# Row maxima of the first batch's scores taken ahead of a block's hidden product on VectorE

## What is computed

```python
def ffn(x):        # 8 experts, top 2
    scores = softmax(xt @ router_w); weights, idx = top_k(scores, 2)
    h = gelu(x @ w1[e]) * (x @ v1[e])        # D = 128, F = 352
    y = h @ w2[e]
    return sum_k weights_k * y[idx_k] + bias
def attn(x):       # 16 heads of 8
    q, k, v = rope(qkv)
    attn = q @ k.T * scale + alibi
    out = softmax(attn) @ v
    return out @ proj_w.T + proj_b
x = x + 0.5 * ffn(layernorm(x))
x = x + attn(layernorm(x))
x = x + 0.5 * ffn(layernorm(x))
```

## Time and profile before

| | |
|---|---|
| median of three runs | 499.47 us |
| the profiled execution's own time | 502.36 us |
| its span, first to last instruction | 500.5 us |
| TensorE busy in the span | 439.6 us (88%) |
| TensorE weight loads | 367.2 us (73%) |
| VectorE | 318.6 us (64%) |
| ScalarE | 249.1 us (50%) |
| GpSimd | 236.9 us (47%) |
| mean granted TensorE clock | 0.972 |

### The profile page before, as it was taken

The page is one execution under the profiler, slowest core; times in us unless marked ns, Lnnn a source line. Parts: engine busy times, 40 slices in busy tenths (PEclk is TensorE's granted clock), DMA queues, the critical chain, the costliest instruction groups (busy, mean ns, idle before and its releaser), DMA issues.

```text
span 500.5 us, 10906 instructions
## 1 busy us (share of the span) xinstructions
PE 439.6 (88%) x3447; PEld 367.2 (73%) x3447; DVE 318.6 (64%) x935; ACT 249.1 (50%) x585; POOL 236.9 (47%) x321
## 2 busy tenths in 40 slices
PE   1999989989889884998989898989788999999990
PEld 1878878888878663676867676767557988888880
DVE  3767869778556645384868585847436675545672
ACT  4745644364443534354565546454664554554441
POOL 7267796564523214034435253514254568643341
PEclk9999999999999989798999899999998999999996
DMA  9981121223220102121212111110022123223522
GB/s 245 284 116 55 48 75 45 79 71 97 70 60 24 43 22 54 33 65 34 55 53 54 45 48 40 45 43 22 7 87 64 53 67 112 59 60 96 149 79 79
DMA packets 50633, 35.51 MB, mean 71 GB/s; under 512 B 5754, under 2 KB 47706, under 8 KB 50538
## 3 DMA queue, kind: packets, MB, share of 16 engines
q1 hardware_dynamic: 45140, 23.90, 19.3%
q0 software_dynamic: 4784, 10.54, 6.3%
q10 hardware_dynamic: 656, 0.40, 0.3%
HBM read 15.37 MB, written 13.01 MB: 57 GB/s over the span
## 4 chain that ended last, share of the span: by engine, by line
PE 58%; DVE 8%; issue 7%; ACT 5%; POOL 4%; DMA 3%; ACTq 1%; SPq 1%; POOLq 0%; DVEq 0%
PE bank L1582 6%; PE bank L1485 5%; PE bank L1606 5%; PE bank L1621 5%; PE bank L1478 5%; PE bank L1467 4%; PE bank L1468 3%; PE bank L1469 3%; PE bank L1585 3%; PE bank L1586 3%; PE bank L1609 2%; PE bank L1610 2%; POOL yp L538 2%; PE bank L1457 2%; DVE nm L1260 2%
## 5 line engine op out<-in xcount | busy, mean ns | idle before, releaser
L538 POOL DMA_INDIRECT yp<-scr,dest x77 | 76.5, 994 | 90.2 <-ACT scr L768 63.1
L1260 DVE TENSOR_REDUCE nm<-bank 128x2 f32<-128x512 f32 x128 | 83.9, 685 | 46.6 <-PE bank L1586 45.1
L875 ACT ACTIVATE stage<-bank 128x512 f32<-128x512 f32 x128 | 75.2, 596 | 68.8 <-PE bank L1610 68.1
L1485 PE MATMUL bank<-wd,scr 128*128 (+1 forms) x462 | 64.2, 275 | 1.3 <-ACT scr L761 1.3
L1467 PE MATMUL bank<-wu,xbT 128*128 x154 | 62.3, 405 | 2.1 <-DVE xbT L1126 1.8
L1134 DVE COPY scr<-bank 128x256 f32<-128x256 f32 x77 | 32.5, 423 | 46.8 <-PE bank L1478 46.3
L1485 PEld LDWEIGHTS bank<-wd,scr 128*128 128x128 f32 (+1 forms) x462 | 60.0, 191 | 1.8 <-issue 1.7
L1582 PE MATMUL bank<-qk_rows 126*128 126x256 bf16 x256 | 51.4, 283 | 5.5 <-DVE nm L1260 5.5
L1606 PE MATMUL bank<-qk_rows 128*128 128x256 bf16 x256 | 50.9, 282 | 2.4 <-DMA qk_rows<-wd 2.0
L781 ACT ACTIVATE scr<-bank 128x352 f32<-128x352 f32 x77 | 35.7, 464 | 32.4 <-PE bank L1469 32.1
L1469 PE MATMUL bank<-wu,xbT 128*128 x154 | 50.2, 326 | 0.0
(11 more groups left out here) (218 smaller groups left out, 958.7 us busy)
## 6 DMA issues: line engine op xcount, KB each, us to landing
qk_rows<-lev SPq DMA_DIRECT2D x96, 64.0 KB
scr<-xs SPq DMA_DIRECT2D x77, 64.5 KB, 1.9
stage<-yp SPq DMA_DIRECT2D x8, 256.0 KB, 4.1
scr<-yp SPq DMA_DIRECT2D x6, 256.0 KB, 2.9
stage<-in_w SPq DMA_DIRECT2D x8, 176.0 KB, 3.7
stage<-in_v SPq DMA_DIRECT2D x8, 176.0 KB, 5.1
xs<-qk_rows SPq DMA_DIRECT2D x3, 451.5 KB, 11.1
yp<-scr,dest POOLq DMA_INDIRECT x77
```

The lines of the kernel that those rows point to most:

```text
L538: nc.gpsimd.indirect_dma_start(out=yp[PHASE[n]][:, :], out_offset=bass.IndirectOffsetOnAxis(ap=dest[:, n:n + 1], axis=0), in_=ysb[:, n % Y ...
L875: nc.scalar.activation(probs[:, g % RING, kt, 2 * (hp % 2):2 * (hp % 2) + 2, :], psS2[(b * 16 + j) % 3][:, :].rearrange("p (h n) -> p h n" ...
L1260: nc.vector.tensor_reduce(nm[:, qt, 2 * hp:2 * hp + 2], psS1[i % 2][:, :].rearrange("p (h n) -> p h n", h=2), AX.X, ALU.max, negate=True). ...
L1485: i = nc.tensor.matmul(ph[n % len(ph)][:, 3 * P:4 * P], hTs[0:w, n % 2, k * P:(k + 1) * P], wd[0:w, bass.ds(experts[n], 1), k, :].rearrang ...
```

## The change

VectorE takes the maxima of turn n - 1's units directly behind the hT copy, ahead of its wait for the gelu and the second up product. It took them at the end of the turn. The same maxima are taken in the same turn; nothing else moves, and only the first feed-forward's blocks are affected.

```diff
                 for n in range(first, last + 1):
                     if n > first:
                         hT_copy(r, n - 1)
+                        if r == 0:
+                            for i in s1_early(n - 1):
+                                row_max(0, i)
                     if n < last:
                         dve.wait_ge(gelu_done, n + 1)
                         dve.wait_ge(v_full, n + 1)
...
                 for j in near_parts(n):
                     near_low(j // H, j % H)
-                if n:
-                    for i in s1_early(n - 1):
-                        row_max(0, i)
                 if n == 30:
                     max_low(0)
```

## The result

The changed kernel takes 493.76 us (median of six runs, 493.3 to 495.15) against 499.71 for the kernel before in the same comparison (six runs, 499.25 to 504.58, the three of the table ahead among them). The ratio is 0.9862, 95% interval 0.982 to 0.9903: 5.95 us between the medians, where 4.7 were forecast. The profiled execution took 494.26 us with a span of 492.4; before it was 502.36 and 500.5, 8.1 more. So there are three answers, 4.7 forecast, 6.0 in the medians and 8.1 between two profiles, and the experiments have to say what belongs to the change.

The account below looks back on a forecast made before the run. TensorE bounds blocks 17 to 30, with holes waiting for VectorE's maxima. 1.20 + 4.00 - 0.47 - 0.03 = 4.70 us comes off the 499.47 us median, giving 494.8 us, range 492.8 to 496.9.

Parts of the forecast that it names:

- The bound: Blocks 17 to 30: TensorE sets the pace, its holes are waits for VectorE's maxima; time saved there comes off the end.
- A blocks: Blocks 18, 21, 24, 27, two score units, the second needing this turn's first maximum: gain 0.30 us each, 1.20 in all.
- B blocks: Blocks 19, 22, 25, one score unit needing this turn's first maximum, plus an xbT split: gain 1.33 us each, 4.00 in all.
- Turn 28: Block 28 has two maxima but no score to cover them, so the next transposes load later: loss 0.47 us.
- The slip behind B blocks: The later product delays the next block's transpose load by 0 to 0.05 us each, at most 0.15 in three; 0.03 taken.
- cover: Delay a product can take before TensorE's next transposes come later: 0.22 us in S, 0.70 in A, -0.05 in B blocks.
- The first rival, the overlap lost: VectorE's maxima and product run end to end without the 0.08 us overlap: gain 4.0 us, 495.5 us; chance 0.09.
- The second rival, the clock: Attention meets one low clock stretch more (496.5 us, chance 0.12) or fewer (493.1 us, 0.06), at most 1.7 us.
- The third: Gain taken back behind the blocks by a transfer bound to an earlier moment: 499.5 us, or half, 497.1; chance 0.05.
- fourth: Slower: VectorE's delayed product holds TensorE's next transposes with nothing covered: 1.6 us slower, 501.1 us; chance 0.04.
- S: Blocks 17, 20, 23, 26, one score unit whose maxima are long done: no wait for the delayed product, block 2.42 us.

Follow-up runs that it names:

- after_again: The changed kernel unchanged, run a second time for another profile: median 494.08 us of six runs, ratio 0.9896 to before; 40.55 us from block 17 to the attention.
- before_again: The kernel before, unchanged, run again for a second profile: median 498.52 us of 12 runs; 45.33 us from block 17 to the attention.
- only_a: Against the kernel before, maxima taken early only in turns 18, 21, 24 and 27: 496.95 us, one run; 44.13 us from block 17 to the attention.
- only_b: Against the kernel before, maxima taken early only in turns 19, 22 and 25: median 495.39 us; 41.35 us from block 17 to the attention.
- keep28: The changed kernel, but turn 28's two maxima stay behind the product: median 496.57 us, 493.73 when repeated; 40.06 us from block 17 to the attention.
- dose_all: The changed kernel plus two clears of an unused tile between maxima and product in turns 19 to 27: 500.57 us, one run.

## Why the prediction was right

**The bound** was right: TensorE with holes at the maxima, and nothing behind the blocks bound to anything but their end. The first product of the attention came 4.8 us sooner against block 17, and the time behind it, 328.3 us in after_again, is that of before_again (328.2).

**A blocks**: 4 x 0.30 forecast, 1.20 measured alone (only_a). **B blocks**: 4.00 forecast, 3.98 alone (only_b), 2.77 forecast for a block and 2.76 measured. **Turn 28**: loss 0.47 forecast, 0.49 by keep28 (0.44 in the block itself). **The slip behind B blocks**, 0 to 0.05 each, 0.03 taken in all: in blocks 20, 23 and 26 the load slips by 0.02 to 0.03, to 0.35 or 0.36 into the block, and the matmul stays at 0.49, so TensorE lost nothing. The cover there is -0.04 by the dose, so the room was used up to the last few hundredths. The sum for the blocks was 4.70 and measured 4.80.

**The first rival, the overlap lost**: in the B block above the copy, the two maxima and the product start 0.34, then 1.19 (two maxima) apart, and the block's product ends at T + 3.06 where end to end would give T + 3.33. The overlap of 0.08 holds with a maximum ahead of a product. The Trainium skill ("VectorE: DVE Perf Modes", "The DRAIN you can't avoid") says that the next operation does not start until the pipe is empty. The trace does not agree with the strict reading of it, by which each pair would be 0.08 further apart. By the overlap lost the gain would have been 4.0 instead of 4.7.

**The second rival, the clock**, is where the miss of 1.0 us most likely lies, as far as the record goes. The forecast gave one low stretch more or less 18% of the chance and 1.7 us. In fact the single execution scatters by more: before from 497.5 to 502.3 in before_again's own runs, with 21.8 to 28.0 us low. The profile on which I made the sum was one of the longer ones (28 us low, 502.36 against a median of 499.47), which the prediction noted as "2.9 below" without asking why. That did no harm, because the clock is at its high level in the blocks in every profile. So the 4.7 for the blocks was right for the reasons given, and 0.1 short. What was sized too small is the chance given to the clock: the median came 1.0 us under the forecast, inside the range, and that it moved this way and not the other is not something the prediction can claim.

**The third and fourth rivals** fall: the time behind the blocks did not take anything back, and S and A blocks have 0.23 and 0.69 us of cover. The 2.07 us of the earlier trace rows, the prediction's example for the fourth, is a weak one: what released the matmul there was ScalarE's copy L768, behind an hT copy that itself came late, and the change leaves the hT copy in its place. The dose is the better evidence.

## What to carry to other kernels

When an in-order engine holds a result that frees a buffer for TensorE behind a product that waits for TensorE, take the result first; what it costs is the delay of the product beyond its cover, which can be read as the distance from the product's end to the weight load that needs it. Do that sum for each kind of turn: TensorE lost nothing in eleven turns here and 0.44 to 0.49 us in the one that had no score to cover it. And when a profile is microseconds away from the median, look at its granted clock before using its length; compare two kernels by a stretch that repeats to 0.02 us rather than by their ends.

## What the runs showed of the hardware

The scatter of this kernel's time goes with TensorE's clock: 0.47 us for each us at the 1.2 GHz level over 90 runs, with 18 to 38 us of it per execution. This is a relation between runs and not an experiment on the clock. Some 8 us of it lie behind the last matmul (484.2 to 492.4 us in the change's profile), where they cost nothing. The others in that profile (from 102, 191, 324 and 372 us on) lie behind gaps of TensorE or stretches in which it had little to do. The same gap does not always lead to one: behind the gap of 2.1 us that starts at 100.0 us in both profiles of before, the clock is low for 3.4 us in the second (from 103.5 on) and stays high in the first.

VectorE instructions in the block's chain that wait for nothing still open start 0.08 us before the one ahead has ended: a copy and a maximum, two maxima, a maximum and a product. This is not so for every pair. The 64-partition product L1252 and a maximum behind it start 0.03 us behind the end (184.20, 0.69 long, then 184.92 in the change's profile, and so in all six such pairs), and the first clear in dose_all starts 0.05 to 0.06 us behind the end of the maximum. Where the second instruction waits for the first by a semaphore, 0.17 us pass between them (the two clears of dose_all).
